# A sixteen-head attention regrouped: one head of four batches in a step, three rounded products for queries and output, projections reordered

## The reference, cut to what matters

```
ik, mk = input_seq @ Wk + bk, state_seq @ Wk + bk      # input_seq: context
iv, mv = input_seq @ Wv + bv, state_seq @ Wv + bv      # state_seq: layernorm(x)
q = einsum('bmd,hdp->bhmp', state_seq, Wq) + bq         # 16 heads of 128 features
inp_score = einsum('bhmp,bsp->bhms', q, ik)
self_score = sum(q * mk[:, None], -1)
attn = softmax(concat([self_score, inp_score]) / sqrt(128))
heads = einsum('bhms,bsp->bhmp', attn[..., 1:], iv) + attn[..., 0:1] * mv
attn_out = concat_heads(heads) @ Wo + bo
x1 = layernorm(attn_out + state_seq); mlp(x1)
```

## Time and profile before

| | |
|---|---|
| median of 3 runs | 939.27 us (939.08 to 939.92) |
| the profiled execution, its time | 941.33 us |
| its span, first to last instruction | 939.6 us |
| busy over the span: PE, DVE, ACT, POOL | 776.7, 556.9, 408.3, 388.7 us |
| mean granted clock of PE | 0.841 of 2.4 GHz |
| first `queries` on DVE to last | 251.82 to 417.88 us |

### The profile page before, as it was taken

One profiled execution on the slowest core, in us unless ns is written; L12 is line 12 of the kernel. 1 busy time (PEld: TensorE's weight loads), 2 busy tenths in 40 slices (PEclk: granted clock), 3 DMA queues, 4 the chain that ended last, 5 costly groups with the idle time before them and its releaser, 6 DMA issues. The chain is left out here.

```text
span 939.6 us, 16171 instructions
## 1 busy us (share of the span) xinstructions
PE 776.7 (83%) x4962; PEld 661.4 (70%) x4962; DVE 556.9 (59%) x1471; ACT 408.3 (43%) x1263; POOL 388.7 (41%) x366
## 2 busy tenths in 40 slices
PE   4888579999799999996839999667745999998655
PEld 2566469998589999995729788345534888886654
DVE  5655565444566666666445777557764556665555
ACT  1754134442045445453223677177621446664202
POOL 4642221220333443442221677388625058875100
PEclk9555579999789999998958999855666999999578
DMA  4000001113000000000002444000001032210000
GB/s 152 2 1 1 24 12 46 45 36 121 6 1 2 2 0 0 1 0 1 1 23 70 140 139 154 0 1 2 1 1 57 4 122 93 76 46 1 0 1 23
DMA packets 14274, 33.06 MB, mean 35 GB/s; under 512 B 1744, under 2 KB 5864, under 8 KB 13952
## 3 DMA queue, kind: packets, MB, share of 16 engines
q1 hardware_dynamic: 14208, 32.26, 10.1%
HBM read 31.63 MB, written 0.62 MB: 34 GB/s over the span
## 5 line engine op out<-in xcount | busy, mean ns | idle before, releaser
L1118 PE MATMUL banks<-input_hi,weights_in_lo 128*128 128x512 f32 x280 | 117.3, 419 | 22.8 <-PEq L1437 12.9
L918 ACT ACTIVATE probabilities<-banks,neg_max 128x128 f32<-128x128 f32 x256 | 90.0, 376 | 60.7 <-ACTq L915 60.7
L1118 PE MATMUL banks<-input_lo,weights_in_hi 128*128 128x512 f32 x280 | 113.5, 405 | 0.0
L1118 PE MATMUL banks<-input_hi,weights_in_hi 128*128 128x512 f32 x280 | 113.2, 404 | 0.0
L1118 PEld LDWEIGHTS banks<-weights_out,hidden 128*128 128x128 f32 x864 | 102.0, 194 | 3.2 <-DVE hidden L2105 1.0
L1118 PE MATMUL banks<-weights_out,hidden 128*128 128x128 f32 x864 | 102.7, 278 | 0.7 <-ACT att_feat L1040 0.7
L666 POOL TENSOR_TENSOR rstd<-var_eps,neg_half 128x4 f32<-128x4 f32 x24 | 25.2, 1049 | 163.1 <-POOLq L665 147.0
L987 ACT ACTIVATE hidden<-banks,cols 128x512 f32<-128x512 f32 x80 | 54.6, 689 | 70.5 <-ACTq L985 70.4
L958 ACT ACTIVATE probabilities<-banks,neg_max 128x128 f32<-128x128 f32 x128 | 45.3, 366 | 90.4 <-ACTq L956 90.4
L1118 PEld LDWEIGHTS banks<-input_hi,weights_in_lo 128*128 128x128 f32 x280 | 55.1, 197 | 37.0 <-issue 22.4
L837 POOL TENSOR_TENSOR scratch<-values_state,self_weight 128x512 f32<-128x512 f32 x32 | 33.3, 1042 | 102.5 <-POOLq L828 96.6
(11 more groups left out here) (238 smaller groups left out, 1832.8 us busy)
## 6 DMA issues: line engine op xcount, KB each, us to landing
scratch<-cw_rows SPq DMA_DIRECT2D x19, 512.0 KB, 3.8
weights_out<-w_in SPq DMA_DIRECT2D x17, 256.0 KB, 3.0
weights_in<-w_in SPq DMA_DIRECT2D x8, 512.0 KB, 3.6
weights_in<-w_in SPq DMA_DIRECT2D x9, 256.0 KB, 3.1
weights_in<-w_in SPq DMA_DIRECT2D x16, 128.0 KB, 2.2
weights_out<-w_in SPq DMA_DIRECT2D x16, 128.0 KB, 2.1
wq<-w1q_in SPq DMA_DIRECT2D x1, 1024.0 KB, 6.2
wo<-w1o_in SPq DMA_DIRECT2D x1, 1024.0 KB, 8.5
```

Source lines behind the costliest of these rows:

```text
L918: act.activation(prob[:, n // 2 % 2, h, :], b8(n % 3)[:, i, :], ACT.Exp, bias=neg_max8[:, n % 4, i:i + 1], accum_out=z[:, n // 2 % 2, h:h ...
L1118: return pe.matmul(o, l, rh, start=start, stop=stop, **kw)
```

## The change

A step becomes one head of four batches, so `queries` and `output` have one weight and 512 tokens: each becomes three rounded products of 512 columns. For that ACT rounds the weights (`round_heads`) and POOL makes their low parts (`low_heads`, four of 128x1024, three of them in steps 1, 2 and 4). The turned heads are rounded too: ACT makes the high part (`round_headsT`), DVE the low part (`low_headsT`, every step). The sums of 16 heads come out turned, so ACT copies them and PE turns them back (`copy_sums`, `turn_sums`, twice in all). `residual` is done twice, for four batches each. The norm of the first half for the MLP moves to steps 23 and 24 of DVE, the split of the MLP's weights and the bias on xn to POOL inside the loop. The 32 steps are written out without a loop. At the entry the context's keys are projected before the last output of the network before is freed, ACT evacuates the keys, and the second half of the state projections (`state_rest`) stands behind the first `queries`. SP loads wq1 and wo1 at the start.

```
+        wq_hi = (in_hi[:, 1, :], w_hi[:, 1, :])
+        wq_lo = (in_lo[:, 1, :], w_lo[:, 1, :])
+        wo_hi = (w2_hi[:, :, :].rearrange("p a t -> p (a t)"), h_hi[:, 6:8, :].rearrange("p a t -> p (a t)"))
+        wo_lo = (w2_lo[:, :, :].rearrange("p a t -> p (a t)"), h_lo[:, 6:8, :].rearrange("p a t -> p (a t)"))
...
-            load_experts(w0_in, ffn0)
+            sp.wait_ge(rows_loaded, 16)
+            sp.wait_ge(sq_rest_loaded, 16)
             sp.dma_start(wq1[:, :, :], w1q_in).then_inc(w1_attn_loaded, 16)
             sp.dma_start(wo1[:, :, :], w1o_in).then_inc(w1_attn_loaded, 16)
+            load_experts(w0_in, ffn0)
...
+            def low_heads(raw, hi, lo, k, count):
+
+                pool.wait_ge(attn_rounded, count)
+                pool.tensor_tensor(lo[k], head_group(raw, k), hi[k].bitcast(F32), ALU.subtract)\
+                    .then_inc(attn_split, 1)
...
-                pipelined(pool, [(self_values, range(8), 2), (self_products, range(8), 0)],
-                          8, NB // 2, lambda: None)
...
+                pipelined(pool, [(lambda it, n: inverse_roots((0,)), (15,), 8), (self_values, range(32), 2),
+                                 (self_products, range(32), 0),
+                                 (lambda it, n: low_heads(wq1, wq_hi, wq_lo, 1, 2), (1,), 0),
+                                 (lambda it, n: low_heads(wo1, wo_hi, wo_lo, 0, 3), (2,), 0),
+                                 (lambda it, n: low_heads(wo1, wo_hi, wo_lo, 1, 4), (4,), 0),
+                                 (add_row, (6, 8), 0), (mlp_weights, (12, 14, 16, 18), 0)],
...
-            inverse_roots()
-            split_weights(mlp1, 0)
+            inverse_roots((0,))
+            low_heads(wq1, wq_hi, wq_lo, 0, 1)
+            inverse_roots((1,))
             wide_attention()
-            inverse_roots()
+            inverse_roots((1,))
             mlp_rows()
...
+            def round_heads():
+
+                act.wait_ge(w1_attn_loaded, 32)
+                for raw, hi in ((wq1, wq_hi), (wo1, wo_hi)):
+                    for k in range(2):
+                        act.activation(hi[k], head_group(raw, k), ACT.Copy).then_inc(attn_rounded, 1)
...
+                def round_headsT(it, n):
                     act.wait_ge(headsT_done, 1)
                     act.sem_inc(headsT_done, -1)
-                    act.activation(headsT[:, n % 2, :, :], b4(5), ACT.Copy).then_inc(headsT_ready, 1)
+                    act.activation(headsT_hi[:, n % 2, :], bank[5][:, :], ACT.Copy).then_inc(headsT_hi_ready, 1)
+
+                def copy_sums(it, n):
+                    act.wait_ge(wo_done, 1)
+                    act.sem_inc(wo_done, -1)
...
-                pipelined(act, [(copy_headsT, range(8), 5), (copy_probsT, range(8), 3), (exps, range(8), 1)],
-                          8, NB // 2, st.close)
+                pipelined(act, [(round_headsT, range(32), 5), (copy_probsT, range(32), 3),
+                                (copy_sums, (15, 31), 6), (exps, range(32), 1)], 32, 1, st.close)
...
-            evacuate_transposed(xnT)
+            round_heads()
+            evacuate_keys(kT, 2)
+            act.wait_ge(st.sem, st.n)
+            act.sem_inc(keys_ready, 1)
+            take_tokens(4)
+            evacuate_keys(qT, 2)
+            act.wait_ge(st.sem, st.n)
+            act.sem_inc(state_keys_ready, 2)
+            act.sem_inc(keys_ready, 1)
+            st.close()
...
+                        pe.wait_ge(attn_split, 1 + n // 8)
                     pe.wait_ge(q_free, 1)
                     pe.sem_inc(q_free, -1)
-                    for i in range(4):
-                        m = mm(b4(0)[:, i, :], wq1[:, 4 * (n % 4) + i, :],
-                               xnT[:, bass.ds((2 * it + n // 4) * P, P)])
-                    m.then_inc(heads_q_done, 1)
+                    split_products(bank[0][:, :], lambda part: head_part((wq_lo, wq_hi)[part], h),
+                                   lambda part: (in_lo, in_hi)[part][:, 0, tokens], True, True)\
+                        .then_inc(heads_q_done, 1)
+
+                def state_rest(it, n):
+
+                    pe.wait_ge(feat_ready, 1)
+                    pe.sem_inc(feat_ready, -1)
+                    project(w("wk1"), xnT, 2, (1,), projected_act)
+                    project_tok(w("wv1"), xnT, 4)
 
                 def scores(it, n):
+                    if n == 0:
...
                 def values(it, n):
+                    if n == 0:
+                        pe.wait_ge(state_values_read, 1)
+                        pe.sem_inc(state_values_read, -1)
+                    else:
+                        pe.wait_ge(heads_ready, 1)
                     pe.wait_ge(probsT_ready, 1)
                     pe.sem_inc(probsT_ready, -1)
                     for i in range(4):
-                        m = mm(b4(4)[:, i, :], probT[:, 0, 4 * (n % 2) + i, :],
-                               iv[:, bass.ds(2 * it + n // 4, 1), :].rearrange("p a b -> p (a b)"))
+                        m = mm(b4(4)[:, i, :], probT[:, 0, 4 * (n % 2) + i, :], iv[:, n // 16 * 4 + i, :])
                     m.then_inc(pv_done, 1)
...
                 def turn_heads(it, n):
                     pe.wait_ge(heads_ready, 1)
                     pe.sem_inc(heads_ready, -1)
+                    if n > 0:
+                        pe.wait_ge(headsT_ready, 1)
...
                 def output(it, n):
+                    h = n % 16
                     pe.wait_ge(headsT_ready, 1)
                     pe.sem_inc(headsT_ready, -1)
-                    if n % 4 == 0:
-                        pe.wait_ge(wo_free, 1)
-                        pe.sem_inc(wo_free, -1)
+                    if n in (0, 8):
+                        pe.wait_ge(attn_split, 3 + n // 8)
+                    if n == 16:
+                        pe.wait_ge(y_copied, 1)
+                    m = split_products(bank[6][:, :], lambda part: head_part((wo_lo, wo_hi)[part], h),
+                                       lambda part: (headsT_lo, headsT_hi)[part][:, n % 2, :],
+                                       h == 0, h == H - 1)
+                    if h == H - 1:
+                        m.then_inc(wo_done, 1)
+
+                def turn_sums(it, n):
+                    pe.wait_ge(y_copied, 1)
+                    pe.sem_inc(y_copied, -1)
                     for i in range(4):
-                        h = 4 * (n % 4) + i
-                        m = mm(bank[6][:, 0:D], headsT[:, n % 2, i, :], wo1[:, h, :],
-                               start=(h == 0), stop=(h == H - 1))
-                    if n % 4 == 3:
-                        m.then_inc(wo_done, 1)
+                        t = pe.transpose(b4(3)[:, i, :], y_wide[:, i * P:(i + 1) * P], ident[:, :])
+                    t.then_inc(y_turned, 1)
 
                 pe.sem_inc(q_free, 1)
-                pe.sem_inc(own_free, 1)
-                pe.sem_inc(wo_free, 1)
-                pipelined(pe, [(queries, range(8), 0), (scores, range(8), 1), (output, range(8), 5),
...
-                pipelined(pe, [(queries, range(8), 0), (scores, range(8), 1), (output, range(8), 5),
-                               (turn_heads, range(8), 4), (values, range(8), 3), (turn, range(8), 2)],
...
-            project(w("wk1"), ctxT, 2)
-            project_tok(w("wv1"), ctxT, 4)
-            transpose_tiles(xn)
+            project(w("wk1"), ctxT, 2, (0, 1), projected_act)
+            pe.wait_ge(y_free, 4)
+            pe.sem_inc(y_free, -4)
+            transpose_half(0, xn, 4)
+            project_tok(w("wv1"), ctxT, 6)
+            transpose_half(1, xn, 5)
+            pe.wait_ge(keys_ready, 1)
+            pe.sem_inc(keys_ready, -1)
             pe.wait_ge(feat_ready, 1)
             pe.sem_inc(feat_ready, -1)
-            pe.wait_ge(qkv_ready, 1)
-            pe.sem_inc(qkv_ready, -1)
-            project(w("wk1"), xnT, 2)
-            project_tok(w("wv1"), xnT, 4)
-            pe.wait_ge(qkv_ready, 1)
-            pe.sem_inc(qkv_ready, -1)
-            pe.wait_ge(w1_attn_loaded, 32)
...
                 def queries(it, n):
                     dve.wait_ge(heads_q_done, 1)
                     dve.sem_inc(heads_q_done, -1)
-                    at = COLS["bq1"][0] + 4 * (n % 4)
-                    dve.tensor_tensor(qh[:, n % 2, :, :], b4(0),
-                                      cols[:, at:at + 4][:, :, None].broadcast_to([P, 4, P]), ALU.add)\
+                    dve.tensor_scalar(scratch[:, n % 2, :], bank[0][:, :], col("bq1", n % 16), None, ALU.add)\
                         .then_inc(st.sem, st.one())
                     dve.wait_ge(st.sem, st.n)
                     dve.sem_inc(qh_ready, 1)
                     dve.sem_inc(qh_ready_pool, 1)
                     dve.sem_inc(q_free, 1)
+
+                def state_values(it, n):
+                    copy_values(mv, 4, "bv1")
+                    dve.wait_ge(st.sem, st.n)
+                    dve.sem_inc(state_values_ready, 1)
```

(47 more changed lines are left out.)

138 lines of the change are left out of this document (110 added, 28 removed).

## The result

| | before | after |
|---|---|---|
| median | 939.6 us (939.08 to 940.91, 4 runs) | 960.28 us (956.61 to 962.13, 4 runs) |
| ratio | | 1.0213, 95% interval 1.0181 to 1.0246 |
| profiled execution: time, span | 941.33, 939.6 us | 962.13, 960.4 us |

A forecast was written before the change was run, and what follows sets the result against it. DVE with its hand-over gaps (5.30 us a step) and PE (5.34) were taken to bound the loop within 1%. Terms 10.9 + 5.5 - 8.9 - 0.7 = +6.8 us on 939.27 gave 946.1 us, range 941 to 951 (934 to 957 with rivals 2 to 4).

The forecast's parts named there:

- The sum: Whole kernel: loop +10.9, moved work +5.5, entry and start -8.9, exit -0.7, together +6.8 us.
- The exit: Last queries to the MLP's first product: norm's 4.4 us gone, 3.7 added, -0.7 us, between -4 and +4.
- The entry's two terms: First queries on DVE 7.4 us sooner; the five steps up to step 5 take 24 us for 25.6.
- the moved work: First half's norm, 4.4 us, in steps 23 and 24, and first four batches' residual, 1.1, cost the DVE-bound loop +5.5 us.
- DVE step: Attention loop: 5.13 + 0.64 low part + 0.05 bias = 5.82 us a step, 10.9 us more over 26 steps.
- rival 1: Loop: DVE's gaps are real waits and close, PE bounds at 4.86 us a step; 919 us, chance 0.15.
- rival 3: Loop: low parts cost 0.95 us a step or come late, 6.13 us a step; 954 us, chance 0.12.
- PE's step: Attention loop: rounded queries and output, 0.69 us each, bring PE's step from 5.34 to 4.86 us.
- both lie within what DVE does meanwhile: Loop: PE's step 22 wait for bank 3 and products delayed by POOL's step 23 root, claimed hidden behind DVE's work.
- Rival 4: Loop: PE, idle 1 us in 5.8, gets 1.2 GHz in parts, some 8 us more; 954 us, chance 0.05.
- The norm of 4.4 is gone from it: Exit: moving the first half's norm into the loop was credited with its whole 4.4 us.

The follow-up runs named there:

- e2: Changed kernel, with the last operation of all four DVE stages signalling the consumers itself, without own-counter waits, separate increments and consumers' decrements: 939.0 us, ratio 0.9998 to the kernel before.
- b2: Kernel before the change, with two of DVE's four hand-overs a step (heads, self weights) signalled by the last operation itself: 937.95 us, ratio 0.9986.
- e3: Changed kernel, with output as one f32 product a head, wo not rounded and no low part of the turned heads on DVE: 939.82 us, 0.9992 of the kernel before.
- e4: Changed kernel, with the second half of the last network's input transposed and split where the kernel before did it: 953.65 us, 1.0167 of the kernel before.
- e5: e4's kernel, with the first half's norm and POOL's roots moved from loop steps 23 and 24 into the drain: 952.07 us, 1.0128 of the kernel before.
- e6: Changed kernel, with POOL's inverse roots of the first half placed behind the self values and self products of their step: 960.63 us, 1.0242 of the kernel before.
- e9: e4's kernel, with DVE's low part of the MLP's first input half put ahead of the second half's norm: 955.2 us, 1.0172 of the kernel before.
- b1: Kernel before the change, with one more 128x512 DVE operation behind the queries in each of 32 steps, result unused: 952.74 us, ratio 1.0149.
- e7: Changed kernel, with f32 output, all DVE hand-overs on the last operation, the last network's half restored and POOL's roots behind the products: 931.0 us, 0.9896 of the kernel before.

## Why the prediction was right in its direction and wrong in its size

The sum missed by 14 us in the stretches of the profiled executions. The exit is 3.9 us worse than forecast, the last network 3.1, the entry 3.0, the stretch behind the MLP's first product 2.7, the moved work 1.8, and single longer steps of the loop 1.2, whose cause I didn't follow. The loop's ordinary steps are 1.6 better. (The entry's two terms make 9.0, where the sum took 8.9.)

**The loop: right.** The DVE step was forecast at 5.82 and is 5.76 (the queries' TENSOR_SCALAR 0.75, no gap behind the low part). Rivals 1 and 3 fell. e2 shows that the gaps are the price of waiting for one's own counter and of the increments: with the same data on every engine, taking them away removed 21 us. e2 takes away the consumers' decrements too, but b2 leaves those in place, and its two gaps go all the same. The Trainium skill's sentence ("VectorE: DVE Perf Modes", "The DRAIN you can't avoid": "the semaphore costs nothing extra here") I had stretched too far. e2 agrees with it: a semaphore that the last operation increments adds no gap. What costs 0.26 to 0.47 us, four times a step, is to wait for that semaphore on DVE itself and to send the increments as instructions of their own; the runs don't tell these two apart.

**PE's step: wrong, harmless to the sum.** 4.86 was forecast, e2 shows 5.16. I multiplied the 0.23 of the earlier trace rows, which stands between rounded products in a row, by three; behind an f32 product the first takes 0.31 and the last is followed by up to 0.37 until the f32 values start. With DVE at 5.76 it cost nothing; it shows in PE's idle time, 3.4 of 50 us, less than half of the 1 us a step that was forecast. It makes rival 1 worth less than I said, by 26 x 0.30 = 7.8 us. e2 is its loop, and with the exit and the last network on top it comes to 939, not 919.

**The work that moves into the loop: 5.5 forecast, 7.3 measured.** DVE's rows of steps 22 to 24 in the changed kernel split it. The residual costs 1.1, as forecast. The norm costs 1.6 for its statistics and 2.6 for its application, 4.2 for 4.4. The failed sentence is "both lie within what DVE does meanwhile", which put two waits at nothing. PE's wait for bank 3 is 2.0 us long, the clock falls behind it, and the next queries come 0.5 late for DVE. POOL's root delays its products of step 23, and that costs 1.4:

```profile
383.22 1.04 POOL L694 TENSOR_TENSOR rstd<-var_eps,neg_half 128x4 f32<-128x4 f32 x1 [8.41 <-POOLq L875]
...
385.23 1.26 POOL L867 TENSOR_TENSOR scratch<-scratch,queries_feat 128x512 f32<-128x512 f32 x1
```

```profile
388.78 0.69 DVE L2066 TENSOR_REDUCE row_max<-banks 128x4 f32<-128x512 f32 x1 [1.67 <-DVEq L2063]
```

PE idles 2.83 us for that product of POOL, until 386.79, and its products with `ones` then take 1.83 us in place of 1.02, at a granted clock of 0.50; DVE waits 1.67 ahead of its maxima, where 0.26 is usual. Rival 4's mechanism, a clock that falls in part of the loop, was real behind these two idles, in a small form.

**The exit: -0.7 forecast, +3.2 measured.** This is the step that failed most, in two of its terms. The first is "The norm of 4.4 is gone from it", which credits its whole length. But in the kernel before, the norm began at 435.79 beside the last `turn_heads` and `output`, and PE's output product there is done late:

```profile
435.85 0.63 PE L1297 MATMUL banks<-identity,scratch 128*128 128x128 f32 x4 [0.49 <-PEq L1295]
437.35 1.13 PE L1118 MATMUL banks<-wo,scratch 128*128 128x128 f32 x8 [0.87 <-PEq L1302]
```

It ends at 438.48, and the residual came at 440.21; only the last 1.5 us or so of the norm lay on the path. That is an estimate from these rows; no run takes the norm out of the kernel before.

The second is the low part, of which the sum has one, at 0.94 us. e3, which has no low parts, has an exit 4.5 us shorter: 2.0 up to the last heads and 2.5 behind them. Together the two terms are off by more than 3.9; without the low parts the drain up to the last heads is also 1.7 shorter than before (15.0 for 16.6), which the sum did not count. After the change DVE's timeline of the drain reads:

```profile
446.56 1.13 DVE L2099 SCALAR_TENSOR_TENSOR scratch<-banks,inverse_sums,scratch 128x128 f32<-128x128 f32 x4 [0.80 <-DVEq L2097]
447.95 0.69 DVE L2058 TENSOR_TENSOR hidden_lo<-banks,hidden_hi 128x512 fp32r<-128x512 f32 x1 [0.26 <-DVEq L2057]
450.22 0.69 DVE L2058 TENSOR_TENSOR hidden_lo<-banks,hidden_hi 128x512 fp32r<-128x512 f32 x1 [1.58 <-DVEq L2057]
454.77 0.69 DVE L2113 TENSOR_TENSOR att_tok<-xn_tok,banks 128x512 f32<-128x512 f32 x1 [3.87 <-DVEq L2112]
```

From the last heads to the MLP's first product at 459.50 it is 12.9 us; before, 434.52 to 444.55, 10.0. In e3 it is 10.5, close to 10.0 less 1.5 for the norm plus 2.1 for the copy, the transposes and the wider residual, so these additions were sized well. The low part there is a chain through four engines (turned heads, ACT's high part, DVE's low part, PE) whose every link is waited for: 1.58 ahead of the low part and 3.87 ahead of the residual.

**The last network: 3.1 us that the sum left out.** The change also rewrites `second_half_at`, a line that isn't among those printed above, and the prediction doesn't mention it. e4 shows the 3.1 to be this line's.

**The entry: right within its scatter.** -5.6 and -0.4 for -7.4 and -1.6. The code up to there is the same in e4, e5, e6 and e9, and their profiled executions have -7.6, -6.6, -6.5 and -6.9 to the first queries, and 24.0 to 24.1 up to step 5, where I took 24. The sum of -8.9 stands against -8.0 to -9.1 in these four and -6.0 in the changed kernel's own.

**Left open.** From the MLP's first product to the second store of `cw_rows` the changed kernel takes 2.7 longer. 2.1 of it lie in the attention of layer 2, whose code is the same, and there the time goes with the granted clock. From its context projection on PE to that store it takes 160.8 to 160.9 us at 0.69 (the kernel before, b1, e3, e9) and 161.6 to 163.7 at 0.65 to 0.67 (all others, b2 among them, which doesn't have the change). Why an execution gets the one or the other clock no run shows, so I don't count it as a cost of the change. The other 0.6 us are in the MLP's stretch, and there the code is not the same: the edit of `second_half_at` moves the second half of the MLP's input too, and e4 leaves that as it is. PE idles 2.38 us there, as in the last network:

```profile
470.34 0.47 PE L1229 MATMUL banks<-input_hi,weights_in_lo 128*128 128x512 f32 x1 [2.38 <-PEq L1511]
```

No run puts it back, and what it costs is not shown. Part of e4's other 3.5 us goes with the clock of the MLP's stretch; the rest has no cause shown.

## What to carry to other kernels

Before costing an edit, find each engine's step with its fixed gaps in it, not its busy time: here the engine with a third of its time idle was the bound, one operation of 0.7 us a step on it cost 13 us, and letting the last operation signal the consumer gave 21. Work taken from one place counts only by what of it was on the path there, and work put ahead of something that another engine waits for, a bank or a product, costs that engine's wait and what its clock loses. Look up every caller of a rule that a diff touches.

## What the runs showed of the hardware

**DVE behind POOL.** In e7 the operation that turns the row maxima into the negated ones takes 1.01 us in 25 of the 32 steps, under 0.2 in 26 and 29 of the steps of the kernels before and after. DVE's timeline of e7, then POOL's:

```profile
323.81 1.01 DVE L2063 TENSOR_SCALAR neg_max<-row_max 128x4 f32<-128x4 f32 x1
```

```profile
323.53 1.27 POOL L872 TENSOR_TENSOR scratch<-scratch,queries_feat 128x512 f32<-128x512 f32 x1
```

It ends at 324.82, with POOL's product at 324.80. In nearly all steps of all the kernels here it ends 0.02 to 0.07 us behind the product of POOL that it starts beside, so its time is set by when it starts. The 128x512 `queries` operation, which reads PSUM, doesn't show this: ten of the changed kernel's 32 start while POOL is busy, and all 32 take 0.74 to 0.75. The Trainium skill, page "SBUF — State Buffer", section "Who interferes with whom", has a port pair that DVE in some modes and POOL lock for a whole instruction; the rows agree. It cost nothing in e7, whose PE has no idle time, but it took back what e6 had gained, and 1.1 us in e5.

**PE's clock.** An idle of 2.0 us in the middle of a loop at 2.4 GHz was followed by products 0.43 apart in place of 0.23, at a granted clock of 0.61 for the 4.4 us that followed (e5, windows above). One of 2.8 us in the changed kernel was followed by 4.2 us at 0.50 (386.8 to 391.0). The idles of 0.2 us in each step of the changed kernel were followed by no such fall: its window has 1.00.
